# Opening of a selective-scan kernel: one unit's chain ahead of the scans, the other chunks prepared inside units 0 to 2, first dt and du loaded by channel quarters

## The chip, the cores and the metric

One core of one Trainium2 chip. The metric is the device time of one execution in microseconds, as the median of several runs.

## What is computed

The reference, cut: 4096 tokens (2 sequences of 2048) are looked up in an embedding table (a slice of 64 columns), normalised, and go through a bidirectional Mamba block and then a top-1 mixture of 32 small experts, each with a residual.

```python
h = table_slice[x]                                   # (2, 2048, 64)
# attention block, on layernorm(h)
proj = layernorm(u, ln_g, ln_b) @ in_w.T             # 64 -> 256
conv_input, gate = split(proj)
act = silu(dwconv_causal(conv_input, conv_w, conv_b))   # (.., 128)
for way in (forward, backward):                      # mamba(act) and flip(mamba(flip(act)))
    x, z = split(act @ in_w.T); x = silu(dwconv_causal(x, ...))
    dt = softplus(x_dbl[..., :R] @ dt_w.T + dt_b)    # x_dbl = x @ xproj_w.T, R = 8
    h_t = h_{t-1} * exp(dt_t * A) + dt_t * x_t * B_t # 128 channels x 16 states
    y_t = sum_n h_t[n] * C_t[n] + x_t * D
    out = (y * silu(z)) @ out_w.T
h = h + concat(fwd, bwd) * silu(gate) @ out_w.T + residual
h = h + experts(layernorm(h))
```

## The kernel before, in words

The sequence is cut into chunks of T = 512 tokens, 4 chunks (CB) in each of the 2 sequences. A **unit** is one chunk in one direction; there are 16 (UNITS), in order: way f of sequence 0 (units 0 to 3), way b of it (4 to 7), then the same for sequence 1. A unit has 16 scans: the 128 channels x 16 states are laid out as 16 tiles of 128 partitions x 512 steps, (r, q) with r = 0..3 (state group) and q = 0..3 (a quarter of 32 channels; the 128 partitions hold 4 states m of 32 channels d).

Each engine runs a list that is written out by hand, and the engines meet in semaphores that only count up. For one unit u:

- **SyncE (SP)** copies dt and du (dt times x) of the unit, which lie as channels x time, to DRAM, and loads them back spread to the scan's layout: `dtS` and `duS`, 128 x (4 quarters) x 512, 1 MB each. `load_dt` (L344) and `load_du` (L351) do it with four copies, one for each state m, each writing 32 partitions. `load_B` and `load_C` (L365, L374) spread the rows of B and C in the same way into `repB` and `repC`. All these tiles have two buffers.
- **ScalarE (ACT)** makes the decays exp(dt x A) with one instruction for each (r, q) (`decay`, L988) into one of three PSUM banks, so at most three ahead of the scans. Between them it does the pieces of `between` (L1044): the softplus of unit u + 2 in five steps, square and reciprocal root of layernorms, and at the end of a unit `burst` (L1032), the silus of x and z of unit u + 3 between two loads of the function table.
- **VectorE (DVE)** runs the scans (`scan`, L1339) and, for r = 1 and 3, the products dt x B from PSUM (`input_product`, L1332), and the small work of its own `between` (L1414).
- **GpSimd (POOL)** makes the products for r = 0 and 2 (`input_product`, L450), multiplies the scanned states by C (`by_c`, L457) for all r, and does three steps of the softplus (`softplus`, L437). In unit 0 DVE has r = 0, 1, 3 (`on_dve`, L101).
- **TensorE (PE)** does all projections and convolutions (as four products with shifted inputs), sums the states (`sum_states`, L643), and `add_nought` (L637) issues products that add zero.

Ahead of the unit loop lies the opening. POOL gathers the tokens (tiles 0 to 20), waits for the softplus of unit 0, gathers the rest, fills constants, and does the softplus of unit 1 (L466 to L480). DVE goes through the layernorms of chunks 0 to 3 one after the other (L1298 to L1310), then constants. PE and ACT prepare all four chunks of sequence 0 (turned input, act, gate), the convolution and x of units 0 to 2 and their z, the softplus of units 0 and 1 (L759 to L782 and L1121 to L1181). Only then ACT and POOL pass `constants_ready` and the loop begins. Every layernorm shares one set of small PSUM columns in the bank ZED and one buffer `xc`. The chunks of sequence 1 are prepared one a unit, in units 1 to 4. SP loads the weights of way f, of way b and of the experts (`late_loads`) first, then for units 0 and 1: stores, dt, du, B, C.

## Time and profile before

| | us |
|---|---|
| median of 3 runs | 606.04 |
| lowest, highest | 605.75, 606.38 |
| the profiled execution | 607.73 |
| its span (first to last instruction) | 605.9 |

| engine | busy us | share |
|---|---|---|
| PE (matmul) | 480.8 | 79% |
| VectorE | 483.3 | 80% |
| ScalarE | 357.5 | 59% |
| GpSimd | 517.9 | 85% |

The profile is of one execution; times in it count from the first instruction. Busy time does not contain waiting for semaphores or issuing of DMAs. Each product of 128 x 2048 takes GpSimd 4.53 us and VectorE 2.27 us; a scan of 128 x 512 takes 1.27 us; a decay 0.68 us. "Idle before" in a row names the instruction whose semaphore ended the wait.

### The profile page before, as it was taken

How to read it: one execution, taken by the hardware profiler on the slowest of the kernel's cores; microseconds unless marked ns; L12 is line 12 of the kernel's file. 1: busy time of each engine (PE TensorE's matmuls, PEld its weight loads, DVE VectorE, ACT ScalarE, POOL GpSimd, SP SyncE). 2: the span in 40 equal slices, each digit the busy share in tenths (PEclk: the TensorE clock that was granted, in tenths of full speed). 3: DMA queues.
4: the chain of work that ended last, by engine and by line, in shares of the span. 5: the costliest groups of instructions: out<-in, count | busy, mean ns of one | idle time of the engine just before them, and what ended most of it. 6: DMA issues, size and time to landing. Idle time of an engine off the chain costs nothing.

```text
span 605.9 us, 5758 instructions
## 1 busy us (share of the span) xinstructions
PE 480.8 (79%) x1679; PEld 177.7 (29%) x1679; DVE 483.3 (80%) x601; ACT 357.5 (59%) x634; POOL 517.9 (85%) x190
## 2 busy tenths in 40 slices
PE   2576858777788888869888888878887887888897
PEld 1232212232323232314232323232333223323243
DVE  2533069998989896999899889988998899799941
ACT  2454565758585856483857485848574764354533
POOL 5737159999999999999999999999999999989600
PEclk9997958899999897998998999999999998789999
DMA  6839458855555546564644864386429741900000
GB/s 66 33 32 183 84 133 199 192 148 123 152 121 147 130 141 138 144 140 143 138 110 116 190 159 108 98 189 178 109 78 187 195 114 45 207 3 10 9 1 17
DMA packets 51073, 71.32 MB, mean 118 GB/s; under 512 B 16434, under 2 KB 17378, under 8 KB 51042
## 3 DMA queue, kind: packets, MB, share of 16 engines
q1 hardware_dynamic: 48050, 69.63, 47.6%
q0 software_dynamic: 1024, 1.05, 4.5%
q10 hardware_dynamic: 1968, 0.29, 0.3%
q8 instruction: 13, 0.21, 0.2%
q14 instruction: 18, 0.15, 0.1%
HBM read 60.45 MB, written 10.49 MB: 117 GB/s over the span
## 4 chain that ended last, share of the span: by engine, by line
POOL 33%; issue 26%; PE 18%; DVE 15%; ACT 5%; DMA 2%; POOLq 0%; DVEq 0%; ACTq 0%
POOL st L464 16%; POOL st L455 12%; DVE st L1350 9%; DVE st L1337 3%; PE ps L580 2%; PE ps L640 2%; PE ps L646 2%; POOL l_ L441 2%; POOL dt L444 2%; DMA x<-in_L_tok_ple_table,idx 2%; PE ps L627 2%; PE ps L732 2%; PE ps L748 2%; POOL x L429 1%; PE ps L568 1%
## 5 line engine op out<-in xcount | busy, mean ns | idle before, releaser
L464 POOL TENSOR_TENSOR st<-st,repC 128x2048 f32<-128x2048 f32 x63 | 284.9, 4533 | 9.1 <-ACT carry L998 7.8
L1350 DVE TENSOR_TENSOR_SCAN st<-ps,carry,st 128x512 f32<-128x512 f32 x192 | 234.9, 1268 | 19.6 <-ACT carry L998 12.9
L992 ACT ACTIVATE ps<-dtS,negA 128x512 f32<-128x512 f32 x256 | 169.5, 681 | 51.8 <-DVE st L1350 50.4
L455 POOL TENSOR_TENSOR st<-duS,repB 128x2048 f32<-128x2048 f32 x31 | 140.5, 4531 | 0.5 <-PE ps L646 0.5
L640 PE MATMUL ps<-Bw,nought 128*128 128x512 f32 x194 | 103.6, 645 | 0.0
L646 PE MATMUL ps<-st,fold 128*32 128x512 f32 x504 | 69.5, 624 | 42.9 <-POOL st L464 42.7
L1350 DVE TENSOR_TENSOR_SCAN st<-ps,zero,st 128x512 f32<-128x512 f32 x64 | 78.1, 1267 | 3.8 <-POOL st L455 1.9
L1337 DVE TENSOR_TENSOR st<-duS,ps 128x2048 f32<-128x2048 f32 x33 | 75.0, 2271 | 6.3 <-PE ps L627 6.3
L580 PE MATMUL ps<-act,wT 128*128 128x512 f32 x128 | 62.4, 633 | 5.2 <-ACT act L943 5.2
L998 ACT ACTIVATE carry<-st 128x4 f32<-128x4 f32 x48 | 9.8, 204 | 77.7 <-DVE st L1350 77.5
L640 PEld LDWEIGHTS ps<-Bw,nought 128*128 128x128 f32 x194 | 35.6, 202 | 50.0 <-issue 49.9
L627 PE MATMUL ps<-xr,Bw 128*128 128x512 f32 x66 | 38.4, 665 | 6.8 <-DVE lnr L1330 6.0
L441 POOL TENSOR_TENSOR l_<-l_,e_ 128x512 f32<-128x512 f32 x16 | 20.5, 1282 | 26.6 <-DVE e_ L1287 26.6
L429 POOL DMA_INDIRECT x<-in_L_tok_ple_table,idx x32 | 30.5, 952 | 12.6 <-issue 9.1
L646 PEld LDWEIGHTS ps<-st,fold 128*32 128x32 f32 x504 | 10.0, 109 | 95.4 <-POOL st L464 82.1
L580 PEld LDWEIGHTS ps<-act,wT 128*128 128x128 f32 x128 | 25.2, 204 | 35.9 <-issue 29.7
L732 PE MATMUL ps<-xfT,w 64*128 64x512 f32 x64 | 33.9, 610 | 0.0
L1025 ACT ACTIVATE tall<-ps,b 128x512 f32<-128x512 f32 x32 | 21.8, 682 | 17.1 <-PE ps L732 16.9
L1287 DVE SCALAR_TENSOR_TENSOR e_<-ps,e_ 128x512 f32<-128x512 f32 x16 | 10.7, 671 | 22.7 <-ACT l_ L981 22.7
L667 PE MATMUL ps<-wT,ga 128*128 128x64 f32 x128 | 18.1, 286 | 11.3 <-DVE ga L1362 11.3
L601 PE MATMUL ps<-xr,dtproj 128*128 128x512 f32 x32 | 19.8, 704 | 8.7 <-ACT xr L955 8.7
L897 ACT ACT_TABLE_LOAD x16 | 20.5, 1283 | 9.7 <-issue 9.5
(129 smaller groups left out, 590.4 us busy)
## 6 DMA issues: line engine op xcount, KB each, us to landing
dtS<-dt_dram SPq DMA_DIRECT2D x64, 256.0 KB, 6.9
duS<-du_dram SPq DMA_DIRECT2D x64, 256.0 KB, 4.6
repC<-bc_dram SPq DMA_DIRECT2D x64, 256.0 KB, 5.7
repB<-bc_dram SPq DMA_DIRECT2D x60, 128.0 KB, 2.9
dt_dram<-dt SPq DMA_DIRECT2D x16, 256.0 KB, 2.1
du_dram<-du SPq DMA_DIRECT2D x16, 256.0 KB, 2.0
bc_dram<-bc_sb SPq DMA_DIRECT2D x16, 64.0 KB, 5.5
out_h<-fin SPq DMA_DIRECT2D x8, 128.0 KB, 2.0
```

The lines of the kernel that those rows point to most:

```text
L429: pool.indirect_dma_start(out=x0[:, t, :], out_offset=None, in_=rows, in_offset=bass.IndirectOffsetOnAxis(ap=idx[:, t:t + 1], axis=0),).th ...
L441: pool.tensor_tensor(l_[:], l_[:], e_[:], ALU.subtract).then_inc(sem("sp_log1p"), 1)
L455: pool.tensor_tensor(st[:, r], duS[:, u % 2], row, ALU.mult).then_inc(sem("dbu_pool"), 1)
L464: pool.tensor_tensor(st[:, r], st[:, r], row, ALU.mult).then_inc(sem("hc_ready"), 1)
L580: mm = pe.matmul(ps[:, bank, :], conv_wT(way(u), k), act_at(u, 6 - k if way(u) else k), start=(k == 0), stop=(k == 3))
L627: pe.matmul(ps[:, SHORT, :], Bw[:, way(u), r, :], x_of(u), start=True, stop=True) \
L640: pe.matmul(ps[:, Y, :], nought[:], flat(Bw[:, 0]), start=start, stop=False, skip_group_check=True)
L646: mm = pe.matmul(ps[32 * q:32 * q + 32, Y, :], fold[:], st[:, r, q], start=False, stop=(r == NR - 1), skip_group_check=True)
L732: pe.matmul(ps[:, bank, :], w1[:, 8 * k:8 * k + 8, :].rearrange("p e h -> p (e h)"), xfT[0:DM, :], start=False, stop=True).then_inc(sem("h ...
L992: sc.activation(decay_bank(u, r, q), dtS[:, u % 2, q], ACT.Exp, scale=negA[:, way(u), q, r:r + 1]).then_inc(sem("decay_ready"), 1)
L1337: dve.tensor_tensor(st[:, r], duS[:, u % 2], row, ALU.mult).then_inc(sem("dbu_dve"), 1)
L1350: dve.tensor_tensor_scan(st[:, r, q, order], decay_bank(u, r, q)[:, order], st[:, r, q, order], first, ALU.mult, ALU.add).then_inc(sem("sc ...
```

## The change

- VectorE has all four products of unit 0 (`on_dve`), GpSimd none.
- The opening prepares only unit 0 up to its dt and du; VectorE does the arithmetic of its softplus (`first_softplus`) in place of GpSimd. Way b's weights are turned ahead of it. Chunk 1 up to the x of unit 1 follows while the loads are under way, and the last of the four transposed chunks lies just inside unit 0.
- dt and du of unit 0 are loaded by channel quarters q, with a semaphore for each (`first_loads_of`); ScalarE's first decays and VectorE's first products and scans follow quarter by quarter (`first_product`). `load_dt` and `load_du` of all later units have the same form: one copy for each quarter, its source led by four repeats.
- Inside unit 0, in place of `between`, both engines run `first_unit`: softplus of units 1 and 2, act of chunks 2 and 3, x of units 2 and 3, z of unit 0. z of units 1 to 6 and the gates of chunks 1 to 3 are done in the bursts of units 1 to 3 (`zeds`): two z in each.
- Each chunk of sequence 1 is prepared one unit later (2 to 5). `add_nought` does not run in unit 0.
- GpSimd gathers all tokens in one go; the softplus of units 1 and 2 stands inside its unit 0.
- The experts' weights are loaded by SP after the loads of unit 1. Layernorm statistics and `xc` have two buffers (`stat`, `lnr`, `xc[:, n % 2]`).

The diff, cut to its core:

```diff
     def on_dve(u):
         if u == 0:
-            return (0, 1, 3)
+            return (0, 1, 2, 3)
...
+        def zeds(u):
+            return {1: (1, 2), 2: (3, 4), 3: (5, 6)}.get(u, (u + 3,) if u + 3 < UNITS else ())
...
+            def four_times(of, u, q):
+                return of[u][32 * q:32 * q + 32].unsqueeze(0).broadcast_to([4, 32, T])
+
+            def first_loads_of(q):
+                sp.wait_ge(sem("dt_in_dram"), 16)
+                sp.dma_start(dtS[:, 0, q, :], four_times(dt_dram, 0, q)).then_inc(sem(f"dt_first_{q}"), 16)
+                sp.wait_ge(sem("du_in_dram"), 16)
+                sp.dma_start(duS[:, 0, q, :], four_times(du_dram, 0, q)).then_inc(sem(f"du_first_{q}"), 16)
...
-                for m in range(4):
-                    sp.dma_start(dtS[32 * m:32 * m + 32, u % 2], dt_dram[u].rearrange("(q d) t -> d q t", d=32)) \
-                      .then_inc(sem(f"dtS_in_{u % 2}"), 16)
+                for q in range(NQ):
+                    sp.dma_start(dtS[:, u % 2, q, :], four_times(dt_dram, u, q)).then_inc(sem(f"dtS_in_{u % 2}"), 16)
...
-                for m in range(4):
-                    sp.dma_start(duS[32 * m:32 * m + 32, u % 2], du_dram[u].rearrange("(q d) t -> d q t", d=32)) \
-                      .then_inc(sem(f"duS_in_{u % 2}"), 16)
+                for q in range(NQ):
+                    sp.dma_start(duS[:, u % 2, q, :], four_times(du_dram, u, q)).then_inc(sem(f"duS_in_{u % 2}"), 16)
...
-            for u in range(2):
-                store_bc(u)
-                store_dt(u)
-                store_du(u)
-                load_dt(u)
-                load_du(u)
-                load_B(u)
-                load_C(u)
+            store_bc(0)
+            store_dt(0)
+            store_du(0)
+            for q in range(NQ):
+                first_loads_of(q)
+            load_C(0)
+            store_bc(1)
+            store_dt(1)
+            store_du(1)
+            load_du(1)
+            load_B(1)
+            load_dt(1)
+            load_C(1)
+            with nc.allow_non_contiguous_dma(reason="b1 is 2 KB"):
+                for dst, src in late_loads:
+                    sp.dma_start(dst, src).then_inc(sem("late_in"), 16)
...
-            for t in range(TB, TB + 5):
-                gather(t)
-            softplus(0)
-            for t in range(TB + 5, TILES):
+            for t in range(TB, TILES):
                 gather(t)
...
-            softplus(1)
-            pool.wait_ge(sem("constants_ready"), 1)
             for u in range(UNITS):
                 if u:
                     by_c(u - 1, NR - 1)
+                if u == 0:
+                    softplus(1)
                 if 2 in on_pool(u):
                     input_product(u, 2)
                 by_c(u, 0)
-                if u + 2 < UNITS:
+                if 2 < u + 2 < UNITS:
                     softplus(u + 2)
                 by_c(u, 1)
                 if u + 1 < UNITS:
                     input_product(u + 1, 0)
                 by_c(u, 2)
+                if u == 0:
+                    softplus(2)
```

PE's opening and unit 0, as written after the change:

```python
dt_weights(0, 7)
way_b_weights()
turn_chunk(0)
dt_weights(1, 9)
x_chunk(0, 1); conv(0, 1); pre(0); bc(0)
turn_chunk(1); gate_chunk(0, 0); b_rows(0, 0)
x_chunk(1, 1); turn_chunk(2); conv(1, 2); pre(1); bc(1); turn_chunk(3)
b_rows(0, 1); skip_product(0); x_chunk(2, LONG); b_rows(0, 2)
x_chunk(3, ZED); conv(2, PRE); b_rows(0, 3); sum_states(0, 0)
zed(0, ZED, 0); conv(3, LONG); pre(2); sum_states(0, 1); bc(2)
for u in range(1, UNITS):
```

ScalarE inside unit 0, and the end of its burst:

```python
def first_unit(p):
    if p == 1: softplus_in(1); bc_out(1)
    if p == 2: softplus_exp(1); softplus_plus1(1)
    if p == 3: softplus_ln(1); uT_chunk(3)
    if p == 5: keep_last(0, 0)
    if p == 6: silu_tables(); act_silu(2, LONG); act_silu(3, ZED); exp_ln_tables()
    if p == 9: keep_last(0, 1)
    if p == 11:
        silu_tables(); conv_silu(2, PRE); z_silu(0, ZED); conv_silu(3, LONG); exp_ln_tables()
    if p == 13: keep_last(0, 2); softplus_in(2)
    if p == 14: softplus_exp(2); softplus_plus1(2)
    if p == 15: softplus_ln(2); bc_out(2)
```

VectorE ahead of and inside unit 0:

```python
way_taps(0); way_taps(1)
begin_norm(0); norm_var(0); norm_newton(0); start_u2(0); start_residual(0)
way_b_out()
...
begin_norm(1); norm_var(1); begin_norm(2)
norm_newton(1); start_u2(1); start_residual(1); norm_var(2)
first_softplus()                        # log1p_error(0), l - e, dt, du
norm_newton(2); start_u2(2); start_residual(2); begin_norm(3); norm_var(3); rates(1)

def first_unit(p):
    if p == 0: norm_newton(3); start_u2(3)
    if p == 2: log1p_error(1); start_residual(3)
    if p == 3: input_product(0, 1)
    if p == 4:
...

    if p == 5: input_product(0, 2)
    if p == 8: input_product(0, 3)
    if p == 15: log1p_error(2)

for p in range(NR * NQ):
    if p < NQ:
        first_product(p)                # waits du_first_p; one quarter, 128 x 512
    scan(0, p // NQ, p % NQ)
    first_unit(p)
```

## Rows read from the trace of the kernel before

**Rows 1.** Profile page: span, section 1 (busy, instructions), and a group of section 5.
```profile
span 605.9 us, 5758 instructions
...
PE 480.8 (79%) x1679; PEld 177.7 (29%) x1679; DVE 483.3 (80%) x601; ACT 357.5 (59%) x634; POOL 517.9 (85%) x190
...
L429 POOL DMA_INDIRECT x<-in_L_tok_ple_table,idx x32 | 30.5, 952 | 12.6 <-issue 9.1
```

**Rows 2.** Windows: busy us (count) of PE, PEld, DVE, ACT, POOL; PEclk, DMA share, GB/s.
```profile
92.00:565.00 473.00, 390.52 (x1398) 140.82 (x1398) 429.52 (x471) 300.95 (x523) 465.73 (x134) 0.96 0.55 132
113.80:144.60 30.80, 24.68 (x84) 8.66 (x84) 28.92 (x35) 20.92 (x37) 30.64 (x11) 1.00 0.72 170
```

**Rows 3.** Timeline of POOL: start us, us, line, op, tiles, count [idle before <-releaser].
```profile
4.80 1.13 POOL L429 DMA_INDIRECT x<-in_L_tok_ple_table,idx  x1 [3.31 <-DVE idx L1216]
...
79.01 1.26 POOL L441 TENSOR_TENSOR l_<-l_,e_ 128x512 f32<-128x512 f32 x1 [16.48 <-DVE e_ L1287]
...
91.89 4.51 POOL L464 TENSOR_TENSOR st<-st,repC 128x2048 f32<-128x2048 f32 x1 [4.45 <-ACT carry L998]
...
109.26 9.02 POOL L464 TENSOR_TENSOR st<-st,repC 128x2048 f32<-128x2048 f32 x2
```

**Rows 4.** Timeline of DVE.
```profile
13.69 0.43 DVE L1243 TENSOR_REDUCE ps<-x 128x4 f32<-128x256 f32 x1 [3.20 <-DMA x<-in_L_tok_ple_table,idx]
...
40.17 0.69 DVE L1287 SCALAR_TENSOR_TENSOR e_<-ps,e_ 128x512 f32<-128x512 f32 x1 [8.40 <-ACT l_ L981]
...
83.44 1.28 DVE L1350 TENSOR_TENSOR_SCAN st<-ps,zero,st 128x512 f32<-128x512 f32 x1
...
101.39 2.27 DVE L1337 TENSOR_TENSOR st<-duS,ps 128x2048 f32<-128x2048 f32 x1
...
122.45 0.67 DVE L1362 TENSOR_TENSOR ga<-ps,gate 128x512 f32<-128x512 f32 x1
...
141.28 1.28 DVE L1350 TENSOR_TENSOR_SCAN st<-ps,carry,st 128x512 f32<-128x512 f32 x1 [1.57 <-ACT ps L992]
```

**Rows 5.** Timeline of ACT.
```profile
19.18 1.57 ACT L937 ACTIVATE tall<-ps,ln_b,ln_g 64x512 f32<-64x512 f32 x2 [1.72 <-PE ps L547]
...
35.66 1.28 ACT L897 ACT_TABLE_LOAD   x1
...
39.55 0.60 ACT L981 ACTIVATE l_<-ps 128x512 f32<-128x512 f32 x1
...
135.35 1.28 ACT L943 ACT_TABLE_LOAD   x1
```

**Rows 6.** Timeline of PE.
```profile
20.80 3.78 PE L559 MATMUL ps<-tall,wT 128*128 128x512 f32 x4 [1.66 <-ACT tall L937]
...
29.73 5.19 PE L580 MATMUL ps<-act,wT 128*128 128x512 f32 x8
...
51.24 6.45 PE L580 MATMUL ps<-act,wT 128*128 128x512 f32 x8 [5.17 <-ACT act L943]
...
98.41 3.60 PE L580 MATMUL ps<-act,wT 128*128 128x512 f32 x8
```

**Rows 7.** Windows again, for the granted clock inside the second slow group of PE.
```profile
52.00:54.00 2.00, 2.00 (x4) 0.71 (x3) 0.64 (x2) 0.00 (x0) 1.39 (x3) 0.50 1.00 234
```

**Rows 8.** DMA issues from 43 to 60 us: KB each, median us to landing.
```profile
dtS<-dt_dram SPq DMA_DIRECT2D x4, 256.0 KB, 5.4
duS<-du_dram SPq DMA_DIRECT2D x4, 256.0 KB, 8.6
...
dt_dram<-dt SPq DMA_DIRECT2D x1, 256.0 KB, 2.0
```

**Rows 9.** Timeline of SP's queue.
```profile
45.67 1.79 SPq L348 DMA_DIRECT2D dtS<-dt_dram  x4
```

**Rows 10.** Windows again: one store alone, then many loads at once.
```profile
44.00:46.00 2.00, 2.00 (x9) 0.95 (x8) 1.93 (x6) 0.30 (x1) 1.86 (x2) 1.00 0.40 157
86.00:90.00 4.00, 1.92 (x3) 0.29 (x3) 4.00 (x3) 1.84 (x4) 1.44 (x1) 0.50 1.03 223
```

More of the change, by code:

```diff
@@ L238, in build @@
         dt_wT, a = carve(a, 2, P, rows=R)
+        assert a <= 2 * NQ * T
+        pickf, a = carve(3 * NQ * T, NBLK, P, rows=E + 1)
         assert a <= NR * NQ * T
@@ L280, in scan_nth, with spread @@
             return NQ * NR * u + NQ * r + q + 1
+        def spread(u):
+            return 64 * ((u + 1) // 2)
         def x0_of(tile):
@@ L563, in gate_chunk @@
             def gate_chunk(n, bank):
-                if bank == LONG:
-                    pe.wait_ge(sem("act_ready"), n + 1)
-                wait(pe, "gate_ready", n)
+                if n == 0:
+                    pe.wait_ge(sem("wT_copied"), 7)
+                elif n == 1:
+                    pe.wait_ge(sem("x_ready"), 4)
+                else:
+                    pe.wait_ge(sem("act_ready"), CB + 1 if n == CB - 1 else n + 1)
+                    pe.wait_ge(sem("gate_ready"), n)
                 c = n % CB
@@ L1173, in _ @@
-            gate_silu(3, 0)
-            exp_ln_tables()
-            softplus_in(1)
-            softplus_exp(1)
-            softplus_plus1(1)
-            softplus_ln(1)
-            bc_out(1)
-            sc.wait_ge(sem("constants_ready"), 1)
-            sc.wait_ge(sem("gate_ready"), CB)
-            for u in range(UNITS):
+            sc.wait_ge(sem("rates_ready"), 1)
+            def first_unit(p):
+                if p == 1:
+                    softplus_in(1)
+                    bc_out(1)
+                if p == 2:
+                    softplus_exp(1)
+                    softplus_plus1(1)
+                if p == 3:
+                    softplus_ln(1)
+                    uT_chunk(3)
+                if p == 5:
+                    keep_last(0, 0)
+                if p == 6:
+                    silu_tables()
+                    act_silu(2, LONG)
+                    act_silu(3, ZED)
+                    exp_ln_tables()
+                if p == 9:
+                    keep_last(0, 1)
+                if p == 11:
+                    silu_tables()
+                    conv_silu(2, PRE)
+                    z_silu(0, ZED)
+                    conv_silu(3, LONG)
+                    exp_ln_tables()
+                if p == 13:
+                    keep_last(0, 2)
+                    softplus_in(2)
+                if p == 14:
+                    softplus_exp(2)
+                    softplus_plus1(2)
+                if p == 15:
+                    softplus_ln(2)
+                    bc_out(2)
@@ L1183, in _ @@
+            for p in range(NR * NQ):
+                decay(0, p // NQ, p % NQ)
+                first_unit(p)
+            for u in range(1, UNITS):
                 for p in range(NR * NQ):
@@ L1340, in scan @@
                 if q == 0:
-                    if r in on_dve(u):
+                    if u == 0 and r == 0:
+                        pass
+                    elif r in on_dve(u):
                         dve.wait_ge(sem("dbu_dve"), dve_nth[u, r])
@@ L1478, in between, with first_product @@
                     if norm_a(u) is not None:
-                        norm_centre(norm_source(u))
-            input_product(0, 0)
-            for u in range(UNITS):
+                        norm_centre(norm_a(u), norm_source(u))
+            def first_product(q):
+                dve.wait_ge(sem(f"du_first_{q}"), 16)
+                dve.wait_ge(sem("b_ps"), dve_nth[0, 0])
+                if q == 0:
+                    dve.wait_ge(sem("dtproj_ready"), 2)
+                    dve.wait_ge(sem("wT_copied"), 9)
+                dve.tensor_tensor(st[:, 0, q], duS[:, 0, q], ps[:, SHORT, :], ALU.mult) \
+                   .then_inc(sem("dbu_dve" if q == NQ - 1 else "dbu_first"), 1)
+                if q == NQ - 1:
+                    dve.wait_ge(sem("dbu_dve"), dve_nth[0, 0])
+                else:
+                    dve.wait_ge(sem("dbu_first"), q + 1)
+            def first_unit(p):
+                if p == 0:
+                    norm_newton(3)
+                    start_u2(3)
+                if p == 2:
+                    log1p_error(1)
+                    start_residual(3)
+                if p == 3:
+                    input_product(0, 1)
+                if p == 4:
+                    dve.wait_ge(sem("consts"), 1)
+                    ch.mark(dve.tensor_copy(rank[:], ranki[:]))
+                    ch.mark(dve.tensor_copy(pick[:], pickf))
+                    ch.wait()
+                if p == 5:
+                    input_product(0, 2)
+                if p == 8:
+                    input_product(0, 3)
+                if p == 15:
+                    log1p_error(2)
+            for p in range(NR * NQ):
+                if p < NQ:
+                    first_product(p)
+                scan(0, p // NQ, p % NQ)
+                first_unit(p)
+            for u in range(1, UNITS):
                 for p in range(NR * NQ):
```

346 lines of the change are left out of this document (193 added, 153 removed).

## The prediction, made before the change was run

> **What bounds the kernel now.** I read the page first: POOL is the busiest engine [rows 1]. Then windows, to see whether that is an average: from 92 to 565 us POOL works 465.7 of 473 us, and in the stretch of one unit 30.64 of 30.80 us, while DVE has 28.9 [rows 2]. So after 92 us POOL sets the pace, with DVE 2 us behind it. Last the timeline of POOL: its first arithmetic of the steady work stands at 79.01, it waits 4.45 us and is dense from 91.89 [rows 3]. The last group of rows 3 holds two multiplications by C of 4.5 us; the second, that of unit 0, r = 3, begins at 109.26 + 4.51 = 113.8 us. From that instruction on, POOL's list is the same in both kernels: fifteen more units and the tail. **So the change is worth 113.8 us less the new start of that one instruction, less idle time that it adds later.** Everything below works that start out.
>
> **The chain to the first dt.** The first sum of the layernorm stays at 13.69 [rows 4]. Ahead of it now stand the five products of way b's taps (1.2 us); their weights are issued by 10 us and I let them cost 0.5. The first transposed chunk is then in SBUF at 21.3 (19.18 + 1.57 + 0.5) [rows 5]. The x product takes 3.78 [rows 6] to 25.1, its silu 0.7 to 25.8. Before, that silu stood behind the second chunk's layernorm, whose gathers came late, until 29.2. The four convolution products took 5.19 here, 6.45 in a group at the low level (1.2 GHz: granted clock 0.50) and 3.60 at the high one [rows 6, 7]. PE has no longer run before them, so I take 6.0, to 31.8. Silu and table load (1.28 [rows 5]) end at 33.8, a square and a reciprocal root of the later chunks at 34.6, five ScalarE steps of the softplus (3.2 us) at 37.8, where they ended at 40.15 before [rows 5]. Four DVE instructions of 0.67 to 0.69 us [rows 4] replace one on DVE and three of 1.27 on POOL: dt is ready at 40.0, du at 40.7, against 43.6 and 45.0. The store lands 2.0 us later [rows 8], and the first load goes out at 42.0 instead of 45.67 [rows 9]. This part is worth 3.7 us; most of the gain lies behind it, where chunks 1 to 3 no longer stand ahead of the scans.
>
> **The spread of dt and du.** Eight copies of 256 KB, 128 packets of 2 KB each. Every load of before has 32 or more as the leading size on both sides; the new ones have a source that leads with the four repeats. No row shows such a copy, so it needs bounds. Low: it goes as fast as the mass of loads, 223 GB/s [rows 10], 1.2 us a copy and 9.4 for the eight. High: it is cut by its leading size, four engines carry 32 packets each. A packet takes 0.40 x 16 engines x 2 us over 153 packets = 84 ns where a store has the engines to itself, and 1.03 x 16 x 4 us over 435 = 151 ns in a crowd [rows 10]. That is 2.7 to 4.8 us a copy. I take 2.7, for three reasons from the rows: the observed landing of a single copy (5.4 us median with four in flight [rows 8]) is far over 1.2; both sides must be divided alike and the source offers four pieces; and four engines do not fill the 223 GB/s in which the 151 ns arose. Eight copies then end at 42.0 + 21.4, plus 1.3 us for completion (2.0 less the 0.7 of eight packets), plus 2 us in which gathers still share the engines (32 at 1.25 us from 4.80 on end at 45 [rows 1, 3]): the last du quarter is in at 66.5. A page speaks to this: the Trainium skill, "DMA: Bandwidth & Descriptors", section "Why a DMA increments its semaphore by 16 and not by 1", says the number of engines is the largest up to 16 that divides the slowest dimension of both sides, so a leading broadcast of four confines a copy to four engines. By it the sum is the 594.5 below; with sixteen engines it would be the 587 of the first rival. No row of before shows it.
>
> **ScalarE before the scans.** From 37.8 it still does two small ones, the rates of way b, two transposed chunks, gate, act and conv silu, two table loads: 8.7 us of work and 3.7 of waiting for the second convolution, so its first decay could run at 50.2 (53 if that convolution runs at the low level). Quarter 0 arrives near 50 too; quarters 1 to 3 hide ScalarE.
>
> **Unit 0 on DVE.** The last quarter gives product 0.67 and scan 1.27: row r = 0 ends at 68.4 (before, the first scan alone began at 83.44 [rows 4]). Rows 1 to 3 hold 12 scans (15.2), three products of 2.27 (6.8), and the casts and small pieces (1.3): 23.3. Moved into them are the x products of chunks 2 and 3, two convolutions, and on ScalarE two bursts with two table loads each (4.0 and 4.6 us), while the three decay banks cover 3.8 us of scanning. PE has little to do here, unit 0 no longer has its filler products, and the first ones after such a pause run at the low level (6.45 against 3.60 for a convolution [rows 6]): I take 5 us of waiting over both bursts (0 if PE is fast; 8 if each burst waits for a slow convolution). DVE ends unit 0 at 96.7, its piece of unit 2's softplus at 97.4.
>
> **POOL.** Softplus 1, C for r = 0 (its loads queue behind du, near 71), r = 1, the product for unit 1 and C for r = 2 all end by 92 to 94, ahead of that. Softplus 2 is now last of the unit: 3 x 1.27 + gaps = 3.9, to 101.3, and there the instruction of 113.8 stands. **12.5 us are gained.** That unit 0's third product moved from POOL to DVE saves POOL 4.5 us, but before the dense part, so it is in this figure already.
>
> **Units 1 to 3.** The silus of z and gate that are owed are done in their bursts. The burst of one unit took 5.1 us and cost DVE 1.57 [rows 4, 5]; with a second z, through the same bank and so waiting for PE, it takes about 7.2. Unit 1 is eased by 3 us, as the chunk of batch 1 comes a unit later; units 2 and 3 have 2.1 us more. DVE is about 3.4 us ahead of POOL, so I let 1 us through. The late expert weights, the doubled layernorm buffers and the new order of SP's loads I cost at nothing: gathers, POOL's own work and a unit of slack hide them; without that cover the late weights cost the 5 us that SP took to issue them.
>
> **The sum.** 12.5 - 1.0 = 11.5 us. The profiled execution took 607.73 with a span of 605.9 us: it gives 596.2; the median of the runs is 1.7 lower, and the prediction is **594.5 us**. Its own range is 588 to 600.
>
> **Rivals.** (A) The copies use all engines. Row r = 0 is then set by ScalarE's 50.2 and DVE, with a layernorm and softplus piece between, and ends at 61; everything behind it comes 7.4 us earlier: 587. For it: all loads of before run at 223 GB/s; against: the leading size. Chance 0.27. (B) **Slower.** load_dt and load_du have the new form in all sixteen units. If four engines carry them, each has 256 packets of these a unit, and some 66 of the other loads and stores: 322. At 84 ns that is 27 us of the 30.8 of a unit, and hidden; it decides from 96 ns a packet on. At 110 ns it is 35.4, 4.6 us a unit over 15 units less 9 us of slack: 654 us; at 151 ns over 750. For it: the DMA share was already 0.72 in one unit and 0.55 on average [rows 2], and crowded packets take 151 ns [rows 10]; against: a store on otherwise idle engines takes 84. Chance 0.15. (C) Unit 0 and the bursts of units 1 to 3 stall DVE by 8 to 12 us more and POOL, only 2 us above DVE a unit, waits with it: 602 to 607. Against: POOL starts unit 1 behind DVE. Chance 0.10. The forecast keeps 0.48.
>
> **The numbers.** The range takes A's fast end (580, PE fast throughout) and C's far one (606); B is left out with 0.15. A measurement of this kernel can tell about 0.2%, 1.2 us. Faster by more: forecast, A and half of C, 0.80. Same: the other half, 0.05. Slower: B, 0.15.
>
> **What would show it.** First dt load issued near 42; first scan near 51 to 53; last du_first landing near 66 (A: 54), with DMA share near a quarter while they run; row r = 0 ending at 68 (A: 61); the POOL instruction of 113.8 at 101; POOL idle under 3 us behind it. Wrong if DVE or ScalarE wait for dtS or duS in unit 4 or later (B), or if DVE idles over 3 us a unit in units 1 to 3 (C).

## The result and the profile after

The changed kernel takes **711.92 us** (median of four runs, 709.03 to 713.27), against 606.21 for the kernel before, timed beside it: a ratio of 1.174 (95% interval 1.170 to 1.178). It is 17% slower where I forecast 2% faster, and outside the range of 580 to 606. The page of the profiled execution, with the same lines as [rows 1] and the parts that changed most:

```profile
span 711.1 us, 5769 instructions
...
PE 521.7 (73%) x1675; PEld 185.0 (26%) x1675; DVE 490.3 (69%) x608; ACT 359.3 (51%) x636; POOL 511.1 (72%) x186
...
DMA  6984345343534353435345253435353435342000
...
DMA 37%; SPq 21%; PE 16%; DVE 14%; ACT 4%; issue 4%; POOL 3%; DVEq 0%; POOLq 0%; ACTq 0%
...
L490 POOL TENSOR_TENSOR st<-st,repC 128x2048 f32<-128x2048 f32 x63 | 284.7, 4522 | 79.8 <-ACT carry L1053 70.6
...
L1047 ACT ACTIVATE ps<-dtS,negA 128x512 f32<-128x512 f32 x256 | 169.5, 681 | 159.3 <-DMA dtS<-dt_dram 107.6
...
bc_dram<-bc_sb SPq DMA_DIRECT2D x16, 64.0 KB, 12.8
```

POOL has no more work than before: it is busy for 511 us (517.9 in [rows 1]), but of a span that is 105 us longer. DVE has 7 us more. PE has four products fewer and is busy for 41 us more; its mean granted clock in this execution is 0.86, 0.95 in the kernel before. The chain that ended last is no longer POOL's list: 37% of it is DMA and 21% SP's queue. ACT waits 107.6 us for dtS. The DMA digits stand at 2 to 5 tenths in the steady part.

SP's timeline over one period of that part (start us, us that the issues took, line, op, tiles, count), and windows over the same stretch:

```profile
165.74 2.23 SPq L376 DMA_DIRECT2D duS<-du_dram  x4
168.08 10.04 SPq L367 DMA_DIRECT2D dtS<-dt_dram  x4
178.22 6.24 SPq L396 DMA_DIRECT2D repC<-bc_dram  x4
184.50 1.42 SPq L342 DMA_DIRECT2D bc_dram<-bc_sb  x1
197.04 1.72 SPq L389 DMA_DIRECT2D repB<-bc_dram  x4
198.81 0.43 SPq L346 DMA_DIRECT2D dt_dram<-dt  x1
199.28 0.43 SPq L350 DMA_DIRECT2D du_dram<-du  x1
202.62 2.54 SPq L376 DMA_DIRECT2D duS<-du_dram  x4
```
```profile
165.00:169.00 4.00, 2.80 (x11) 1.25 (x11) 4.00 (x6) 2.81 (x5) 3.86 (x2) 1.00 0.11 37
169.00:173.00 4.00, 4.00 (x21) 1.75 (x21) 4.00 (x5) 1.83 (x5) 3.38 (x3) 1.00 0.26 96
...
177.00:181.00 4.00, 1.81 (x5) 0.50 (x3) 3.93 (x5) 2.50 (x5) 3.72 (x2) 1.00 0.26 99
181.00:185.00 4.00, 3.91 (x4) 1.00 (x4) 3.49 (x3) 2.94 (x4) 4.00 (x2) 0.51 0.85 169
...
189.00:193.00 4.00, 4.00 (x12) 0.76 (x11) 0.00 (x0) 1.88 (x2) 0.00 (x0) 0.50 0.26 97
193.00:197.00 4.00, 4.00 (x11) 1.74 (x8) 3.05 (x5) 3.11 (x7) 2.70 (x1) 0.78 0.19 49
```

The period is 202.62 - 165.74 = 36.9 us; a unit of the kernel before took 30.8 [rows 2]. While the eight copies of du and dt run alone, the DMA share is 0.26 and the rate 96 to 100 GB/s: what four engines of sixteen give when they are always busy. At 2 KB a packet, 0.26 x 16 x 4 us over 100 GB/s x 4 us is 85 ns a packet, my 84. The Trainium skill ("DMA: Bandwidth & Descriptors", "Why a DMA increments its semaphore by 16 and not by 1") gives as the number of engines the largest up to 16 that divides the slowest dimension of both sides, and the source's is four here; the trace agrees with its 0.26. Then comes what my rival left out. The store of B and C (184.50) stands behind that backlog, and SP, whose list is in order, can issue nothing more until it has landed: between 189 and 193 POOL and DVE do nothing at all. The profile page gives 12.8 us for that store; before, it was 5.5. SP's list over the same stretch of the kernel before:

```profile
164.22 1.75 SPq L357 DMA_DIRECT2D duS<-du_dram  x4
166.26 1.73 SPq L348 DMA_DIRECT2D dtS<-dt_dram  x4
180.00 3.71 SPq L378 DMA_DIRECT2D repC<-bc_dram  x4
183.76 0.43 SPq L334 DMA_DIRECT2D bc_dram<-bc_sb  x1
188.11 1.71 SPq L371 DMA_DIRECT2D repB<-bc_dram  x4
```

Side by side, one period of the list in us:

| part of the list | before | after |
|---|---|---|
| issuing du | 1.8 | 2.2 |
| issuing dt | 1.7 | 10.0 |
| from there to the first issue of C (before: waiting for POOL) | 12.0 | 0.1 |
| issuing C | 3.7 | 6.2 |
| from the store of B and C to the next issue | 4.4 | 12.5 |
| the rest | 7.3 | 5.7 |
| period | 30.9 | 36.9 |

Two parts grow by 8 us each: SP's own issuing of the four dt copies, and the landing of the store. With C's 2.5 us and du's 0.5 they take the 12.0 us of waiting and, as the rest is 1.6 shorter, 6 us more. The waits of SP's queue over the whole run, before and after (total us, times, longest):

```profile
SPq L378 <- POOL st L464: 116.6, 14, 12.0
SPq L368 <- DMA bc_dram<-bc_sb: 81.6, 14, 10.4
```
```profile
SPq L386 <- DMA bc_dram<-bc_sb: 147.8, 13, 11.9
...
SPq L374 <- DMA du_dram<-du: 40.3, 14, 3.9
...
SPq L396 <- POOL st L490: 10.6, 8, 1.7
```

Before, SP waited for POOL 8.3 us in the mean of 14 units; that was its slack. After, it is 10.6 us in all: the slack is used up, and SP's list of copies sets the pace.

### The profile page after: what moved, and what is told of

Read it like the earlier page. It is cut to its first block, busy times and chain, and to the rows that moved or that the text cites. A ratio compares the mean times of both kernels' runs of the same rounds, so it can differ in the third digit from the quotient of the medians.

```text
span 711.1 us, 5769 instructions
## 1 busy us (share of the span) xinstructions
PE 521.7 (73%) x1675; PEld 185.0 (26%) x1675; DVE 490.3 (69%) x608; ACT 359.3 (51%) x636; POOL 511.1 (72%) x186
## 4 chain that ended last, share of the span: by engine, by line
DMA 37%; SPq 21%; PE 16%; DVE 14%; ACT 4%; issue 4%; POOL 3%; DVEq 0%; POOLq 0%; ACTq 0%
DMA dtS<-dt_dram 27%; SPq L367 11%; DVE st L1462 8%; DMA bc_dram<-bc_sb 6%; PE ps L684 4%; DMA du_dram<-du 3%; SPq L396 3%; PE ps L690 3%; DVE st L1447 3%; ACT ps L1047 2%; SPq L420 2%; POOL st L490 2%; SPq L376 2%; PE ps L648 2%; PE ps L778 1%
## 5 line engine op out<-in xcount | busy, mean ns | idle before, releaser
L490 POOL TENSOR_TENSOR st<-st,repC 128x2048 f32<-128x2048 f32 x63 | 284.7, 4522 | 79.8 <-ACT carry L1053 70.6
L1047 ACT ACTIVATE ps<-dtS,negA 128x512 f32<-128x512 f32 x256 | 169.5, 681 | 159.3 <-DMA dtS<-dt_dram 107.6
L481 POOL TENSOR_TENSOR st<-duS,repB 128x2048 f32<-128x2048 f32 x30 | 135.7, 4522 | 15.7 <-PE ps L690 8.3
L684 PE MATMUL ps<-Bw,nought 128*128 128x512 f32 x188 | 117.7, 743 | 0.0
L690 PE MATMUL ps<-st,fold 128*32 128x512 f32 x504 | 78.1, 696 | 4.2 <-POOL st L490 4.2
L648 PE MATMUL ps<-xr,wT 128*32 128x512 f32 x32 | 25.6, 897 | 64.2 <-DVE st L1447 64.2
L615 PE MATMUL ps<-act,wT 128*128 128x512 f32 x128 | 60.0, 612 | 1.1 <-ACT act L996 1.1
L467 POOL TENSOR_TENSOR l_<-l_,e_ 128x512 f32<-128x512 f32 x15 | 19.0, 1265 | 52.4 <-DVE e_ L1375 52.4
L684 PEld LDWEIGHTS ps<-Bw,nought 128*128 128x128 f32 x188 | 37.5, 223 | 58.4 <-issue 58.4
L671 PE MATMUL ps<-xr,Bw 128*128 128x512 f32 x68 | 38.3, 647 | 14.6 <-DVE st L1600 13.8
L778 PE MATMUL ps<-xfT,w 64*128 64x512 f32 x64 | 38.0, 677 | 0.0
L629 PE MATMUL ps<-act,wT 128*128 128x512 f32 x32 | 20.9, 739 | 15.4 <-DVE x L1371 9.1
L1468 DVE TENSOR_TENSOR zr<-ps,zr 128x512 f32<-128x512 f32 x16 | 11.0, 687 | 29.1 <-PE ps L690 27.9
L690 PEld LDWEIGHTS ps<-st,fold 128*32 128x32 f32 x504 | 10.8, 118 | 66.7 <-issue 55.0
## 6 DMA issues: line engine op xcount, KB each, us to landing
bc_dram<-bc_sb SPq DMA_DIRECT2D x16, 64.0 KB, 12.8
```

What stands on the lines that cost most here:

```text
L481: pool.tensor_tensor(st[:, r], duS[:, u % 2], row, ALU.mult).then_inc(sem("dbu_pool"), 1)
L490: pool.tensor_tensor(st[:, r], st[:, r], row, ALU.mult).then_inc(sem("hc_ready"), 1)
L615: mm = pe.matmul(ps[:, bank, :], conv_wT(way(u), k), act_at(u, 6 - k if way(u) else k), start=(k == 0), stop=(k == 3))
L648: pe.matmul(ps[0:2 * NS, LONG if u == 1 else SHORT, :], wT[:, 15, 2 * NS * way(u):2 * NS * way(u) + 2 * NS], x_of(u), start=True, stop=Tru ...
L671: pe.matmul(ps[:, SHORT, :], Bw[:, way(u), r, :], x_of(u), start=True, stop=True) \
L684: pe.matmul(ps[:, Y, :], nought[:], flat(Bw[:, 0]), start=start, stop=False, skip_group_check=True)
```

## The experiments

Kernels that were timed in one session ran one after another on one chip, with the kernel before among them; every ratio is to the kernel before of the same session.

Two theories at first. **Form:** the copies led by four cost all of it, in any kernel. **Moves:** the new order of SP's list, the bursts and the layout of the opening cost it, and the form does little. First the form alone, in the kernel before:

```diff
-                for m in range(4):
-                    sp.dma_start(dtS[32 * m:32 * m + 32, u % 2], dt_dram[u].rearrange("(q d) t -> d q t", d=32)) \
-                      .then_inc(sem(f"dtS_in_{u % 2}"), 16)
+                for q in range(NQ):
+                    sp.dma_start(dtS[:, u % 2, q, :], four_times(dt_dram, u, q)).then_inc(sem(f"dtS_in_{u % 2}"), 16)
```
(and the same for duS; `du_four`, below, is this edit for duS alone on `wide_all`)

> The kernel before, with one edit: dt and du of all 16 units are spread by quarters, each copy led by four repeats, as in the change; its opening and all else stay. Theory (the new form of these copies is what costs: in the changed kernel four engines carry them at 84 ns a packet, their backlog delays the small store of B and C by 12 us, and SP waits for that store inside its list, which makes a unit 37.5 us long instead of 30.9): 14 to 15 units of 6.6 us more, 695 to 715 us, with the DMA share at 0.26 while dt and du are loaded. Rival (the copies are innocent; the work moved into units 0 to 3 and the bursts cost the time): 604 to 618 us.

Measured 690.67 us, ratio 1.138 (1.133 to 1.144). The form alone costs 85 us (the kernel before took 605.51 beside it). Its SP queue has the same wait in first place:

```profile
SPq L370 <- DMA bc_dram<-bc_sb: 162.3, 14, 12.6
```

Then the reverse: the changed kernel with that form kept for unit 0 only (`wide_later`), and with unit 0's quarters, too, each cut into four copies of 32 rows (`wide_all`):

```diff
-                sp.dma_start(dtS[:, 0, q, :], four_times(dt_dram, 0, q)).then_inc(sem(f"dt_first_{q}"), 16)
+                for m in range(4):
+                    sp.dma_start(dtS[32 * m:32 * m + 32, 0, q, :], dt_dram[0][32 * q:32 * q + 32]) \
+                      .then_inc(sem(f"dt_first_{q}"), 16)
```

> The changed kernel, with load_dt and load_du of units 1 to 15 back in the form of before (one copy for each state m, 32 partitions); the first unit still goes by quarters led by four. Theory (only the form of the later copies costs): the steady unit is 30.9 us again, the first loads still go out at 49 and their last quarter lands near 78; 590 to 602 us. Rival (the moved work costs): 650 us or more.

> As wide_later, and the first unit's quarters too are cut into copies of 32 partitions led by 32 rows, 32 copies of 64 KB in place of 8 of 256 KB. Theory (a copy led by four runs on four engines, one led by 32 on sixteen): the last quarter lands at 49 + 32 x 0.45 us of issuing + 2 = near 66 instead of 78, and the kernel is 5 to 12 us faster than wide_later: 580 to 593 us. Rival (the quarters are slow because the gathers and the store before them are late, not because of their form): within 2 us of wide_later.

`wide_later` took 618.24 us (ratio 1.018, 1.013 to 1.023): 94 of the 106 us are undone. It is 16 us over the top of what I expected of it, so there is a second loss of another kind. `wide_all` took 604.9 (ratio 0.998, 0.995 to 1.001), 13 us less again. The form of the eight copies of unit 0 was worth more than the 7.4 us that rival A gave it. So the form costs nearly all of the 106 us: put into the kernel before it costs 85, taken out of the changed one it gives back 107.

Is it SP's waiting for the B and C store, or that four engines are full? The store was issued on ACT's queue instead:

```diff
-                sp.dma_start(bc_dram[u], bc_sb[:]).then_inc(sem("bc_in_dram"), 16)
+                sc.dma_start(bc_dram[u], bc_sb[:]).then_inc(sem("bc_in_dram"), 16)
```

> The changed kernel, with one edit: the store of B and C goes out on ScalarE's DMA queue in place of SP's, so that it does not stand behind the backlog of the four engines. Theory SP-chain (the 37.5 us of a unit are SP's list in order: 2.3 us of du issues, 10.1 of dt issues, 6.3 of C issues, 12.6 for the B and C store, 6 for the rest): the unit loses most of 12.6 us and falls to the 31 to 33 us of POOL and of the four engines, 610 to 650 us. Rival saturation (the four engines are simply full): no change, 705 to 715 us.

Measured 681.75 (ratio 1.124, 1.118 to 1.129): between the two. The wait went, and another took its place, the wait for du's store:

```profile
SPq L373 <- DMA du_dram<-du: 128.0, 14, 11.0
...
bc_dram<-bc_sb ACTq DMA_DIRECT2D x16, 64.0 KB, 5.0
```

So moving this one store is worth 30 us. On ACT's queue it lands in 5.0 us; the stores of dt and du, still on SP's queue with the copies, take 11.6 and 11.1 us by the profile page, where they took 3.1 and 3.2 in the changed kernel. In both kernels the store that is issued next behind the copies on their own queue is the one that lands late. How the other 76 us divide between such landings, SP's slower issuing and engines that are full, this run does not show. Last, half of the dose: `wide_all` with du of units 1 to 15 in the form led by four, dt wide.

> The wide loads in all units, but du of units 1 to 15 in the quarter form led by four: half of the dose (64 packets on each of four engines a unit, 5.4 us of their time at 84 ns for each copy of two, 10.8 at most for du in all). Theory 'each copy led by four makes SP's list wait for its backlog' (linear in the dose, 106 us between all of it and none): 40 to 60 us slower than the wide loads of the same call, 645 to 665. Theory 'only what does not fit into a unit costs' (dt and du together were 20 to 27 us of the four engines' time, the two B and C loads 10 more, against 30.9): half of the dose fits, and the time is within 10 us of the wide loads, 600 to 620.

656.42 us, against 624.73 for the wide loads in the same session (`wide_all_b`, below): 31.7 us more, between the 10 and the 40 us of my two theories and a third of what the full dose costs (711.9 less 618.2). du has 128 packets on each of the four engines (the 64 that I had written is half of it), 10.8 us; with dt's 32 and the 66 others at 165 ns (below) that makes 27 us of a unit's 30.8, as an estimate. It would fit, and it still costs. By POOL's timeline, where the two are 31 us apart at the end, 9 of them are lost by the last C product of unit 0, where POOL's product for unit 1 starts at 114.26 instead of 105.14; 6 more by unit 7; and 16 in units 8 to 15, where POOL waits 2 to 7 us for du in six of them. SP's list has no slack left; its wait for POOL at the load of C tells it, `du_four` ahead of `wide_all_b`:

```profile
SPq L391 <- DMA bc_dram<-bc_sb: 162.5, 13, 14.3
...
SPq L401 <- POOL st L495: 3.5, 3, 1.3
```
```profile
SPq L402 <- POOL st L496: 95.5, 13, 11.3
```

**The second loss.** The start of the last C product of some units, from POOL's timeline (the fourth of each unit, in unit 15 only its last quarter; unit 0's is the instruction on which my sum rested):

| kernel | unit 0 | 1 | 2 | 3 | 4 | 7 | 15 |
|---|---|---|---|---|---|---|---|
| before | 113.8 | 144.6 | 175.4 | 206.3 | 237.1 | 330.3 | 573.5 |
| after | 117.0 | 156.4 | 194.3 | 225.9 | 269.2 | 378.6 | 678.4 |
| wide_all | 99.2 | 130.6 | 167.7 | 201.2 | 237.0 | 333.9 | 578.8 |
| wide_all_c | 96.4 | 127.3 | 164.1 | 197.1 | 234.2 | 327.3 | 567.7 |

The trace of `wide_all` is of an execution of 613.41 us, 8.5 over its median; that of `wide_all_c`, the same kernel in a later session, of one of 602.29. So the gain and the loss are read from the latter: the opening gains 17.4 us (14.6 in `wide_all`; I had said 12.5), and the units up to 7 give back 14.4 (18.2). The timelines of ACT, PE and DVE in `wide_all` show the burst of unit 1, now with two silus of z and two of gate in one ScalarE table:

```profile
120.83 1.28 ACT L1014 ACT_TABLE_LOAD   x1
...
125.46 0.60 ACT L1021 ACTIVATE zr<-ps 128x512 f32<-128x512 f32 x1 [1.68 <-PE ps L635]
127.47 0.60 ACT L1007 ACTIVATE gate<-ps 128x512 f32<-128x512 f32 x1 [1.41 <-PE ps L608]
128.08 1.28 ACT L956 ACT_TABLE_LOAD   x1
```
```profile
118.16 1.02 PE L635 MATMUL ps<-act,wT 128*128 128x512 f32 x2
...
123.35 2.08 PE L635 MATMUL ps<-act,wT 128*128 128x512 f32 x2 [3.12 <-ACT zr L1021]
125.36 2.07 PE L608 MATMUL ps<-tall,gate_wT 64*128 64x512 f32 x2
```
```profile
126.15 0.43 DVE L1336 TENSOR_REDUCE ps<-x 128x4 f32<-128x256 f32 x1 [2.54 <-issue]
...
130.20 1.28 DVE L1468 TENSOR_TENSOR_SCAN st<-ps,carry,st 128x512 f32<-128x512 f32 x1 [3.16 <-ACT ps L1053]
```

The second pair of products of z waits for the first silu to empty the bank; in those 3.12 us PE does nothing, and then it runs at the low level, 1.2 GHz (2.08 us where the same pair had taken 1.02). The windows give its granted clock, 1.00 ahead of the pause and 0.50 after it:

```profile
117.00:120.00 3.00, 3.00 (x8) 0.92 (x6) 2.96 (x2) 1.63 (x3) 3.00 (x1) 1.00 0.25 77
...
124.00:128.00 4.00, 4.00 (x5) 1.00 (x4) 0.85 (x2) 1.13 (x2) 4.00 (x2) 0.50 0.86 193
```

The burst lasts from 120.83 to 129.38, 8.5 us, and DVE stands for 2.54 + 3.16 = 5.7 us where it stood for 1.57 before [rows 4]. In `wide_all_c` the same burst takes 8.0 us and DVE stands for 5.2. Two edits on `wide_all` try this: one z a burst in units 1 to 5, with the doubles put into units 6, 8 and 10 and the gates left in bursts 1 and 2; and filler products ahead of the second z. A third tries the other lateness, the first load (below).

```diff
-            return {1: (1, 2), 2: (3, 4), 3: (5, 6)}.get(u, (u + 3,) if u + 3 < UNITS else ())
+            return {6: (6, 7), 7: (8,), 8: (9, 10), 9: (11,), 10: (12, 13), 11: (14,), 12: (15,)}.get(u, (u,) if u < 6 else ())
...
+                    if v in (2, 4, 6):
+                        add_nought(3)
...
-            for t in range(TB, TILES):
+            for t in range(TB, TB + 5):
                 gather(t)
...
+            pool.wait_ge(sem("du_in_dram"), 16)
+            for t in range(TB + 5, TILES):
+                gather(t)
```
(the first is `one_z`, the second `warm_z`, the third `gathers_late`)

> wide_all (the changed kernel with all its dt and du copies led by 32), with one edit: the z that are owed are no longer made two to a burst in units 1 to 3; each burst up to unit 5 makes the z of its own unit, and bursts 6, 8 and 10 make two. Theory (what wide_all gives back between 130 and 300 us, 14.5 us ahead of the kernel before at the C product of unit 0, r = 3, and 3.6 behind it seven units later, is lost in the double bursts, where DVE stands 5.7 us each): units 1 to 3 take 31 to 33 us in place of 36 to 37; 590 to 598 us, if bursts 6, 8 and 10 find slack. Rival (the loss is the later chunk work or the order of SP's loads, not the second z): within 2 us of wide_all, 603 to 607.

> wide_all with three products that add zero (3.2 us of PE at its high level) put in front of the second z of bursts 1 to 3, where PE had stood idle 3.1 us and then ran z and gate at 2.07 us each. Theory (half of a double burst's price is PE at the low level): z and gate take 1.1 us there, each burst is 1.5 to 3 us shorter, 598 to 602 us. Rival (the price is the waiting for the bank alone, and the added products stand in the way): 604 to 610 us.

> wide_all with the last eleven gathers moved behind the landing of the first du store. Theory (the store of dt took 8 us to land in place of 2 because 16 gathers more were queued on the engines, and the first load went out at 48 in place of 42): the first load goes out at 42 to 43, row r = 0 ends 4 to 5 us earlier, the kernel is 3 to 5 us faster than wide_all: 600 to 602 us. Rival (what is won there is lost in the bursts, where DVE and not the opening sets the pace): the opening is 5 us earlier and the end within 2 us of wide_all, 603 to 607.

All three missed their expectations: 632.3 (ratio 1.039), 620.6 (1.017), 617.6 (1.013). They ran in another session than `wide_all`, on another chip, and in all three the opening itself was 10 to 18 us later, with stops that no wait of the program explains. So their totals say nothing against `wide_all`; it ran again beside two of them. `one_z` was not repeated.

> The wide loads in all units once more, on the chip that the next two run on. In the three variants timed before, the opening was 10 to 24 us later than in the wide loads, with gaps of 10 us on ACT and PE that no wait of the program explains. Theory 'the edit or where its code lies': here the dt of unit 0 is ready at 39 to 41 us and unit 0's last C product starts at 98 to 101, with a ratio of 0.995 to 1.0. Theory 'chip or execution': the gaps of 10 us are here too, the last C product of unit 0 starts at 108 to 118, and the ratio is 1.01 to 1.03.

> The fillers ahead of the second z once more. If the gaps of the opening belong to the edit (its code is longer by a few instructions per burst), the last C product of unit 0 is at 115 to 118 us again and the ratio is 1.015 to 1.02, while the wide loads without them are at 99. If they belong to the chip, both have the same opening, and this one is 3 to 5 us faster than the wide loads in the same call, by the 4.6 us that units 1 to 4 were shorter.

> The last eleven gathers behind du's store, once more. If the opening's gaps belong to the chip, this one has its first load issued at 41 to 43 us against 48 in the wide loads of the same call, and is 2 to 6 us faster than those. If they belong to the edit, the last C product of unit 0 is at 109 again and the time 1 per cent or more above the kernel before.

The same kernel `wide_all` took 624.73 us here (ratio 1.029, 1.022 to 1.035), with unit 0's last C product at 118.0 instead of 99.2. The stops are not the edits'. Beside it `warm_z_b` took 621.9, 3 us less and within the scatter, and `gathers_late_b` 615.7, 9 us less. What the stops look like, in ACT's timeline of `wide_all_b`, and the same two instructions of the same kernel in a later session (`wide_all_c`):

```profile
35.83 1.57 ACT L996 ACTIVATE tall<-ps,ln_b,ln_g 64x512 f32<-64x512 f32 x2 [9.46 <-remote]
...
49.85 0.69 ACT L1002 ACTIVATE act<-ps,conv_b 128x512 f32<-128x512 f32 x1 [11.14 <-remote]
```
```profile
20.66 1.57 ACT L996 ACTIVATE tall<-ps,ln_b,ln_g 64x512 f32<-64x512 f32 x2 [1.34 <-PE ps L579]
...
25.88 0.69 ACT L1002 ACTIVATE act<-ps,conv_b 128x512 f32<-128x512 f32 x1 [2.35 <-PE ps L595]
```

A first stop of ACT, 6.51 us, ends at 26.03; PE and DVE stand beside it for 5.23 and 4.20 us with no releaser. PE has one of 10.24 us again, to 37.46; for the rest of the time PE and DVE wait for ACT. POOL's gathers meanwhile go on at their even 1.25 us. The last stop ends at 50 us, when the gathers' packets are through (DMA share 0.72 from 40 to 50 us and 0.01 from 50 to 60).

In `gathers_late_b`, where POOL pauses after 21 of its 32 gathers, one stop of this kind is left (8.76 us) and unit 0's last C product is at 105.0, 13 us ahead of `wide_all_b`. The kernel before hardly suffered in these two sessions: its medians are 609.25 and 607.65, against 605.51 and 606.87 in the two others. So whatever its opening met there cost it at most some 4 us, where `wide_all_b` lost 20 against `wide_all`; the changed opening is the more exposed one.

The units' table can be used with the opening taken out: from unit 0's to unit 4's last C product it is 134.1 us in `wide_all_b`, 132.7 and 135.4 in the two of `warm_z`, and 129.2 in `one_z`; from unit 4's to unit 15's it is 338.3 in `wide_all_b` and 348.3 in `one_z`, 10 for three doubled bursts. Unit by unit it can be seen there: up to the C products of units 6, 8 and 10 `one_z`, with a doubled burst just ahead, takes 34.3, 33.4 and 35.0 us, `wide_all_b` 30.9, 30.8 and 30.8. So a second z costs about 3.3 us in those bursts. In units 1 to 3 it costs half as much: with single bursts there `one_z` is 5 us shorter for three, and still 6 over four units of 30.9. What that remainder is, the gates or the later chunks, no run separates. Filling PE ahead of the second z gave little back, though it did keep PE fast. PE's timeline of `warm_z` has the second z of unit 1 at

```profile
141.76 1.13 PE L635 MATMUL ps<-act,wT 128*128 128x512 f32 x2 [0.34 <-ACT zr L1023]
```

The last session was to tell whether the stops come again, whether the kernel before has them too, and whether the gathers can be put out of the way. `gathers_16` is `wide_all` with the fillers of `warm_z`, and with POOL waiting for du's store after the first sixteen gathers:

```diff
+            pool.wait_ge(sem("du_in_dram"), 16)
             for t in range(TB, TILES):
                 gather(t)
```

> The kernel before as it stands, to see the opening on this chip. If the stops of 4 to 12 us in the opening are a matter of chip or execution and come under the gathers, they can fall here too: unit 0's last C product at 113.7 plus 4 to 20 us. If the kernel before is free of them while the wide loads of the same call have them, its units 0 to 3, prepared one after the other ahead of the scans, hide them: its last C product of unit 0 stays at 113 to 116.

> The changed kernel once more, on this chip. In its first profile the dt of unit 0 was ready at 40.7 and the last C product of unit 0 started at 117.0. If the stops under the gathers come with the chip, dt is ready at 55 to 65 here and that product starts at 131 to 140, with the time 10 to 20 us above 712 at most (what POOL's backlog does not take up); the units' period stays at 37 to 38 us. If not, 117 and 712.

> The wide loads as the yardstick of this call. With the stops in the opening: 618 to 625, unit 0's last C product at 115 to 118. Without them: 603 to 606, at 99.

> The wide loads, the fillers ahead of the second z, and the second sixteen gathers behind du's store instead of right behind the first sixteen. If the stops are caused by gathers that run beside the opening's chain: the sixteen end at 24 us, at most one stop of 5 to 9 us is left, dt is ready at 40 to 47, the first load is issued at 42 to 49, and the time is 5 to 14 us below the wide loads of the same call, 598 to 615; a late fourth or fifth chunk (its gathers now end at 47 plus 20 us) may cost 2 to 4 of it. If something else causes the stops, dt is ready at 60 or later and the time is within 4 us of the wide loads.

There are no stops in these four, so they hold no trace of the kernel before under them. `before_again` took 605.82 and `after_again` 707.09 (one execution each), the latter with unit 0's last C product at 114.6: the loss repeats. `wide_all_c` took 605.3 (ratio 0.998, 0.994 to 1.001). `gathers_16` took **601.46** (598.91 to 602.9; ratio 0.989, 0.984 to 0.995), 1.1% under the kernel before, the only variant clearly under it, in a session without stops. SP's timeline shows what the moved gathers change, `gathers_16` ahead of `wide_all_c`:

```profile
40.63 0.34 SPq L346 DMA_DIRECT2D dt_dram<-dt  x1
...
42.67 1.72 SPq L360 DMA_DIRECT2D dtS<-dt_dram  x4
```
```profile
38.36 0.34 SPq L346 DMA_DIRECT2D dt_dram<-dt  x1
...
45.21 1.72 SPq L360 DMA_DIRECT2D dtS<-dt_dram  x4
```

With the gathers running, the first load goes out 6.9 us after the store of dt; without them 2.0. All of that is taken back in unit 0: its last C product is at 96.4 in both. And the two traces, of executions of 602.90 and 602.29 us, reach unit 15's at 568.7 and 567.7. So the 4 us between the medians, at the edge of the scatter, show in no trace, and their cause is open; `gathers_16` also holds the fillers of `warm_z`.

## Why the prediction was wrong

**The step that failed** is the one that put the new form in units 1 to 15 at nothing, rival B's "At 84 ns that is 27 us of the 30.8 of a unit, and hidden; it decides from 96 ns a packet on"; beside it the order of SP's loads stood "at nothing", by "a unit of slack". The copies did run on four engines and at 84 ns, the price at which I called them harmless, and it cost 6 us a unit.

Two things were wrong in it. The 66 packets of the other loads and stores were priced at 84 ns too. In the window from 181 to 185 us, where C's loads run, a packet takes 0.85 x 16 x 4 us over the 330 packets of 2 KB that 169 GB/s makes in 4 us, 165 ns; [rows 10] had shown 151. With 21.5 us for dt and du and 66 x 165 ns = 10.9, it is 32.4 us by this estimate, over the 30.8. And I took the engines as always fed. SP's list is in order and holds three stores whose landing it waits for, so that the four engines are not even full all the time: of the 0.25 that four make, the windows at the two ends show 0.11 and 0.19, which is 2.2 and 1.0 us lost. That makes 35.6 of the 36.9 measured. The table of SP's list gives the same 36.9 from its own side, by durations that were measured: 8.3 us more of issuing for dt and 8.2 more for the landing, against 12.0 of waiting that could be given up.

`du_four` shows that landings and issuing matter by themselves: engine time that by the estimate would fit still cost 31.7 us in all. I had looked for a price from which the rival decides; what I should have read was SP's queue of the kernel before, whose slack was 8.3 us a unit, and asked how much later each landing may come. Of the 117 us by which the forecast missed, 94 are this step (711.9 less the 618.2 of `wide_later`); the rest lies in unit 0 and in units 1 to 3, below.

**Step by step.**
- POOL sets the pace: true of the kernel before and of the wide-load versions; false of the changed one, where POOL waits 79.8 us at its C products.
- The chain to the first dt: dt ready at 40.7 and du at 41.4 (forecast 40.0, 40.7), and at 38.3 and 39.1 in `wide_all_c`; this holds in the sessions without stops.
- "The store lands 2.0 us later [rows 8], and the first load goes out at 42.0": it went out at 48.82. The 2.0 came from a store that was issued at the gathers' end; the new one is issued while they run, and takes 8.1. `gathers_16`, which takes them away, has 42.67.
- The spread: last quarter's product at 78.58 where I had the du quarter in at 66.5 (my own terms add up to 66.7). Seven of the twelve us are the late start. The rest came on with the last quarters: SP issued the last one at 61.18 and C's loads from 63.73 on, with a DMA share of 1.07 from 68 to 72 us, and I had nothing for C there. DMA share 0.23 from 52 to 60 us: the mechanism and its 84 ns were right.
- Unit 0 on DVE: row r = 0 ended at 80.6 (68.4), unit 0's last C product began at 117.0 (101.3; 113.8 before). From the one to the other I had 32.9 us. It is 36.4 in the changed kernel, and 32.2 in `wide_all_c` (64.2 to 96.4), so this part was right where the copies do not disturb it. That 96.4 also lies below my 101.3 is no success of the sum: with wide loads rival A's 7.4 us belong to it, which gives 93.9, and the first load's delay (45.21 for 42.0) is in the difference.
- "The late expert weights ... I cost at nothing", without cover "the 5 us that SP took to issue them": SP issues them from 106.44 to 120.44, 14 us, of which 11.3 go to one copy of `b`. The unit around them takes 39.4 us (117.0 to 156.4), the mean of the fifteen is 37.4; no run separates what they cost.
- "Units 1 to 3": a burst with a second z takes 8.5 us (7.2 forecast), DVE stands 5.7 us in it (about 3.7), and of that 1 us in all was to be let through. In fact the units up to 7 take back 14 us in `wide_all_c` (330.3 - 113.8 before, 327.3 - 96.4 here). This term was mis-sized by 13 us; it takes most of the 17 us by which the opening is ahead there, and the medians keep under 2. The stalls behind the bursts and POOL's waits after them (4.1 us for ACT's carry at 164.08, 5.3 for PE at 206.94) are rival C's mechanism, at rival C's price; the second z is a part of it, and the rest is not taken apart.

**The chances.** B was stated with its mechanism and left at 0.15, since a single packet price spoke against it. The two rows that spoke for it, a DMA share of 0.72 in one unit and 151 ns in a crowd, deserved more.

## What to carry to other kernels

Before a DMA is rewritten into a form that fewer engines carry, count on each of them the packets of a whole period at the crowded price, and then go through the issuing queue in order: how long the issuing itself will take, which store's landing is waited for, what will stand ahead of it, and how much slack the queue has now (its wait for the engine that sets the pace). A copy that overlaps with arithmetic is not hidden if a store that is waited for stands behind it on the same queue. A time gained in the opening has to be followed to the end, since work that was owed there (here the silus of z) comes due in units that have no room for it.

## What the runs showed of the hardware

- **A store under gathers.** A store of 256 KB that lands in 2.0 us [rows 8] took 8.1 us in the changed kernel (issued at 40.68) while POOL's gathers ran. The gathers move little and still keep the DMA engines busy: in `wide_all_b` from 20 to 40 us, with no other traffic, 24 GB/s at a share of 0.82 to 0.89.
- **Stops under gathers.** In two of the experiments' four sessions ACT, mostly with PE and at times with DVE, stood for 4 to 13 us at a time in the first 50 us, in all seven traces of those sessions, and unit 0's last C product came 13 us earlier when eleven gathers were put off. One chip ran one session with and one without the stops, with different kernels whose opening is mostly the same, and `wide_all` itself had them on one chip of three; so it isn't the edit and hardly the chip alone. Gathers take part in it; why it comes in some sessions and not in others stays open.
- **A DVE cast waits for POOL.** The cast of 32 columns of int32 takes 0.18 us in the kernel before. In the changed one it runs beside a POOL product and ends with it (84.96 + 2.48 = 87.44; POOL: 82.90 + 4.51 = 87.41). In `wide_all_c` it is 3.50 us, again to the product's end; in `gathers_16`, where it starts 0.12 us ahead of POOL's product (71.02 and 71.14), it takes 0.19, and that product 4.81 instead of 4.53. DVE's scans beside POOL's products keep their 1.28 us. Why the cast waits stays open. The rows, before and after:

```profile
62.56 0.18 DVE L1317 CAST rank<-ranki 128x32 f32<-128x32 int32 x1 [9.76 <-POOL ranki L478]
```
```profile
84.96 2.48 DVE L1619 CAST rank<-ranki 128x32 f32<-128x32 int32 x1
```
